# Row maxima of the feed-forward weights in units 1, 3 and 5 of each pair of heads, instead of 1, 4 and 7

## What is computed

```
q_r    = rope(q_hk @ w_kc_q) @ W_qr        # per head, rank 64
k_r    = kv @ W_kr                         # per head, rank 64
attn   = softmax(q_r @ k_r.T)              # 256 x 4096 per head
out    = concat((attn @ kv) @ w_kc_kv.T) @ Wo.T
```

```
scale = max(max(abs(row)) / 127, 1e-8)
q     = clip(round(row / scale), -127, 127)
```

## Time and profile before

| what | value |
|---|---|
| median of three runs | 1056.04 us |
| the profiled execution | 1053.18 us |
| its span, first to last instruction | 1051.5 us |
| PE / DVE / ACT / POOL busy | 94% / 70% / 55% / 28% |
| mean granted TensorE clock | 0.994 of full speed |

### The profile page before, as it was taken

How to read it: one execution, slowest core, us unless ns; L and a number is a source line. 1 busy time by engine, 2 the same in 40 slices (tenths; PEclk the granted TensorE clock), 3 DMA queues, 4 the chain that set the end, 5 groups by cost and what they waited for, 6 DMA issues and landing times.

```text
span 1051.5 us, 18010 instructions
## 1 busy us (share of the span) xinstructions
PE 990.6 (94%) x6641; PEld 788.4 (75%) x6641; DVE 732.6 (70%) x1434; ACT 575.1 (55%) x1251; POOL 291.2 (28%) x210
## 2 busy tenths in 40 slices
PE   7989989999998799999998999989899999989996
PEld 5545689999997576687787777878788787968653
DVE  3566456555553789788787888878877787658555
ACT  3445344444443320486776667767676777837633
POOL 6910144444442300000000422313225504013412
PEclk9999999999999999999999999999999999999999
DMA  8560076656632233201113347423323203083010
GB/s 269 130 242 1 4 231 245 213 210 209 209 121 82 83 95 101 71 29 28 52 46 54 61 92 103 91 53 77 76 58 95 72 1 96 8 295 162 1 66 21
DMA packets 65966, 109.18 MB, mean 104 GB/s; under 512 B 19393, under 2 KB 44129, under 8 KB 64738
## 3 DMA queue, kind: packets, MB, share of 16 engines
q1 hardware_dynamic: 65890, 108.17, 35.3%
HBM read 103.24 MB, written 4.91 MB: 103 GB/s over the span
## 4 chain that ended last, share of the span: by engine, by line
PE 76%; DVE 14%; ACT 5%; issue 2%; DMA 1%; POOL 1%; SPq 0%; DVEq 0%; ACTq 0%; POOLq 0%
PE PS L1618 14%; PE PS L1491 12%; PE PS L1607 9%; PE PS L1595 8%; PE PS L1510 5%; DVE scores L1145 3%; PE PS L1580 3%; PE PS L1710 3%; PE PS L1632 2%; PE PS L1339 2%; DVE pL L1198 2%; PE PS L1753 1%; ACT scores L832 1%; PE PS L1391 1%; PE PS L1550 1%
## 5 line engine op out<-in xcount | busy, mean ns | idle before, releaser
L1198 DVE TENSOR_TENSOR pL<-PS,pH 128x512 fp32r<-128x512 f32 x256 | 175.9, 687 | 66.0 <-ACT pH L856 65.5
L856 ACT ACTIVATE pH<-PS 128x512 fp32r<-128x512 f32 x256 | 151.7, 595 | 99.9 <-PE PS L1607 99.9
L832 ACT ACTIVATE scores<-scores,nmX 128x512 f32<-128x512 f32 x256 | 185.2, 723 | 26.3 <-DVE nmX L1149 26.3
L1145 DVE TENSOR_SCALAR_CACHE_REDUCE scores<-PS 128x512 f32<-128x512 f32 x256 | 172.6, 682 | 18.8 <-PE PS L1595 18.4
L1618 PE MATMUL PS<-pH,kvH 128*128 128x256 f32 x512 | 164.4, 321 | 7.4 <-ACT xnT L841 7.4
L1607 PE MATMUL PS<-ident,scores 128*128 128x128 f32 x1024 | 157.3, 276 | 4.5 <-DVE pL L1198 4.3
L1607 PEld LDWEIGHTS PS<-ident,scores 128*128 128x128 f32 x1024 | 117.0, 140 | 36.6 <-issue 16.4
L1618 PE MATMUL PS<-pL,kvH 128*128 128x256 f32 x512 | 143.9, 281 | 0.0
L1618 PE MATMUL PS<-pH,kvL 128*128 128x256 f32 x512 | 143.7, 281 | 0.0
L1618 PEld LDWEIGHTS PS<-pH,kvH 128*128 128x128 f32 x512 | 96.7, 189 | 11.6 <-issue 11.4
L614 POOL TENSOR_TENSOR xn<-xn,winvB 128x1024 f32<-128x1024 f32 (+1 forms) x17 | 39.6, 2330 | 211.0 <-DMA xn<-in_w1t 114.3
(11 more groups left out here) (305 smaller groups left out, 2250.1 us busy)
## 6 DMA issues: line engine op xcount, KB each, us to landing
rawG<-in_wg SPq DMA_DIRECT2D x16, 768.0 KB, 5.7
rawU<-in_wu SPq DMA_DIRECT2D x16, 768.0 KB, 7.2
rawD<-in_wd SPq DMA_DIRECT2D x16, 768.0 KB, 6.4
wrow<-in_w SPq DMA_DIRECT2D x11, 512.0 KB, 5.5
xn<-in_w1t SPq DMA_DIRECT2D x11, 512.0 KB
wturned<-turned SPq DMA_DIRECT2D x4, 1056.0 KB, 13.5
wb<-w_rows SPq DMA_DIRECT2D x32, 128.0 KB, 3.3
wqX<-in_wqX SPq DMA_DIRECT2D x16, 256.0 KB, 2.6
```

The source lines that it names most:

```text
L832: act.activation(at, at, ACT.Exp, bias=nmX[:, p % 2, h, q:q + 1], accum_out=csum[:, p % 2, NT * h + q, c:c + 1]).then_inc(exp_done, 1)
L856: act.activation(pH[:, i % 4], PS[:, 2 + i % 2, :].rearrange("p (k t) -> p k t", t=T), ACT.Copy).then_inc(pH_ready, 1)
L1145: dve.tensor_scalar(sp_[:, h, q, c * CH:(c + 1) * CH], PS[:, 4 * q + h, :], 1.0, None, ALU.mult, ALU.max, accum_out=cmax[:, h, q, c:c + 1] ...
L1198: dve.tensor_tensor(pL[:, i % 4], PS[:, 2 + i % 2, :].rearrange("p (k t) -> p k t", t=T), pH[:, i % 4].bitcast(F32), ALU.subtract).then_in ...
```

## The change

One constant is changed: the units in which a pair's three jobs are done.

```diff
-ROWS_AT = (1, 4, 7)
+ROWS_AT = (1, 3, 5)
```

## The result

The changed kernel takes 1051.1 us (median of 15 runs, 1044.57 to 1057.82), the kernel before 1056.37 us beside it (15 runs, 1052.86 to 1064.52). The ratio is 0.9943, 95% interval 0.9917 to 0.997: 5.3 us less by the medians. 1049.8 us and -6.2 us were forecast.

The account below looks back on a forecast made before the run. PE was taken to bound the kernel, busy 94% of the span and waiting for DVE only where pairs hand over. -7.89 + 0.34 + 0.3 + 1.05 = -6.2 us, from the median 1056.04 to 1049.8 us; range 1045.5 to 1055.5 us.

Parts of the forecast that it names:

- hand-over behind pair 0: Unit 7 and the next unit 0: without the job over 704 columns, 18.63 us falls to 16.58, 2.05 us less.
- hand-overs behind pairs 1 to 4: Unit 7 and the next unit 0: without the third job 1.47, 1.47, 1.45 and 1.45 us less, together 5.84.
- pair 0, units 1 to 6: A job over 704 columns makes a 7.03 us unit 7.37; unit 5 newly pays this, +0.34 us.
- meetings in unit 3, seen in unit 4: Pairs 2 to 4: POOL's first pass holds `wscale`, `add_out` makes PE 0.1 us late each, +0.3 us.
- meetings in unit 5, seen in unit 6: POOL's passes hold `wscale`: pair 2 loses 0.55 us, pair 3 nothing, pair 4 0.5; +1.05 us in all.
- rival 3: Hand-over behind pair 5 is short for another reason; only 0.47 us each is sure: -0.65 us, 1055.4 us; chance 0.13.
- b: DVE's lateness over the usual 0.46 us when the next unit begins; in unit 6, b over 0.75 us is lost.
- Meetings that cost nothing (1): Units 3 and 5: meetings with POOL miss or cost nothing; -7.5 us, 1048.5 us; chance 0.22.
- Meetings at their worst (2): Units 3 and 5: all six hold `wscale` for a whole first pass; +0.2 us, 1056.3 us; chance 0.10.
- That DVE is held for POOL's whole round (4): Units 3 and 5 of pairs 2 to 4: `wscale` loses a whole POOL round; +11.8 us, 1067.8 us; chance 0.05.
- The queues: Next job's row load, issued at most about 9.2 us into unit 3, lands at +15.9, with 3.0 us left.

Follow-up runs that it names:

- Experiments 1: Kernel before with only the second job moved, from unit 4 to unit 3; 1053.98 us, one execution.
- Experiment 5: Kernel before, jobs in units 1, 4 and 7, with the scale made as in experiment 3; 1059.76 us, one execution.
- Experiment 6: Kernel before without the two reductions of the job in unit 7, its small operations kept; 1051.32 us, one execution.
- Experiment 7: Kernel of experiment 3 with both halves behind part 3 in the jobs over 704 columns; 1049.07 us, ratio 0.9931 to the kernel before.
- experiment 9: Changed kernel timed again without new edits; 1052.14 us (12 runs), ratio 0.994 to the kernel before.
- experiment 3: Changed kernel with the scale clamped by a tensor_reduce and multiplied in the accumulator form, instead of the plain tensor_scalar; 1051.34 us, one execution.
- experiment 2: Kernel before with only the third job moved, from unit 7 to unit 6; 1049.4 us, one execution.

## Why the prediction was right

Term by term, in us of loop, from the two traces:

| Term | forecast | measured |
|---|---|---|
| hand-over behind pair 0 | -2.05 | -2.03 |
| hand-overs behind pairs 1 to 4 | -5.84 | -5.73 |
| pair 0, units 1 to 6 | +0.34 | +0.36 |
| meetings in unit 3, seen in unit 4 | 3 x 0.1 | 0.25 + 0.24 + 0.22 |
| meetings in unit 5, seen in unit 6 | +1.05 | +0.76 |
| sum | -6.2 | -5.9 (whole loop -6.05) |

*The hand-over.* It was read from a comparison that the trace of before held already, a pair with the job and one without. Experiments 1, 5 and 6 vary it three ways (job kept, 0.2 us added, 1.2 us removed), and the time followed nearly one for one. That rules out rival 3, by which the hand-over behind pair 5 was short for a reason of its own; so does the 16.6 us that the changed kernel shows behind all five pairs.

*Pair 0.* The three units with a job take 7.38 to 7.39, the others 7.03, as forecast. Experiment 7 shows that another place in the same unit does not help: with both halves behind part 3 the lateness comes out one unit later.

*Unit 3 was mis-sized by a factor of two.* The meeting came where it was put: `wscale` lasted 1.36 to 1.37 us (1.37 expected from 8.83 - 7.46), and in pair 4 the key matmul started 725.39 - 722.91 = 2.48 us into the unit against 2.35 to 2.36 without a hold, 0.12 us late where 0.1 was forecast; in pairs 2 and 3 it was 0.16 and 0.15. The step from the end of `add_out` to the matmul was 0.09 us (724.55 + 0.75 to 725.39), where the prediction had put 0.05. What it left out is that PE loses more than it waits. The matmul behind the wait takes 0.47 us instead of 0.40, and the next starts 0.31 us later instead of 0.23. With this 0.08 the 0.12 to 0.16 us are 0.20 to 0.24, nearly the 0.22 to 0.25 us of the table.

*Unit 5 came out near by luck; how a hold turns into time was right, when it comes was not.* The forecast had pair 2 lose 0.55 and pair 4 half of 0.95. In this execution POOL began pair 2's block 24.5 us after the start of unit 3, not 22.35, and `wscale` was through before it (611.94 against 612.95). The load was issued when forecast (13.62 us, forecast 13.8); what was wrong is the time of the load. The prediction took 8.55 us from the earlier trace rows and called it landing to first use, but it runs from the issue (651.04) to the first use, and here it was 10.9 us, in experiment 9 9.4 us. In the same way pair 4's block took 6.7 and 7.3 us where 5.16 was taken. So `wscale` met L615 there and not L617: b was 1.41, and b - 0.75 = 0.66. A restart as in unit 3, of 0.10, gives the 0.76 us seen. The timeline of pair 4's unit 6 shows the same steps: the tile of part 3 started 6.15 us into the unit (forecast 4.73 + 1.41 = 6.14), and the matmuls of q=1 at 6.89 us, 0.66 behind the 6.23 of before. In experiment 9 it was pair 2 that paid: b = 1.85, 1.10 plus 0.10, seen 1.19. Pair 3, put at 0, had b = 0.41 and lost nothing. So the formula (what DVE is late by, less 0.75) holds in all of these; which pair meets POOL is not settled by the program. The forecast of +1.05 lies between the 0.76 and 1.19 of two executions.

*The other rivals.* Meetings that cost nothing (1) would need unit 4 at 7.88; it took 8.10 to 8.14. Meetings at their worst (2) did not come, the longest `wscale` of the changed kernel being 2.02 us, once. That DVE is held for POOL's whole round (4) is excluded by 722.48 + 1.36, 738.47 + 1.58 and 611.80 + 2.02 = 613.82 beside 611.40 + 2.38 = 613.78: each hold ends with the pass it met.

The Trainium skill ("SBUF — State Buffer", Who interferes with whom) says that the loser of the shared port blocks for the whole instruction and that `tensor_reduce` is outside the lock. The trace agrees with the first: each hold ended within 0.04 us of the POOL pass that it met. It agrees with the second in that `wclamp` took 156 to 157 ns in all fifteen jobs of experiment 3, four of them in the middle of a POOL pass. In this kernel the holds were worth the 1.5 us of experiment 3.

*The queues.* The load of the next job's rows was issued 9.06 us into unit 3 in pair 2 (9.2 at most was forecast), and no job waited for rows: `wscale` stands 7.46 us into units 3 and 5 of pairs 1 to 4 in all cases.

*The total.* The medians differ by 5.3 us where the loop gives 6.05. The interval (0.9917 to 0.997, 3.2 to 8.8 us) holds both. The forecast of 1049.8 us is 1.3 us under the measured median, less than the scatter lets one tell. Whether something of the rest of the span belongs to the change is not settled: it took 569.7 us against 562.2, but experiments 1 (562.3, 11.5 us of its span at the lower clock) and 9 (569.5, 28.7 us) show both values with the same code there, and it goes with the time at the lower clock each time.

## What to carry to other kernels

Where one engine is busy in every stretch but one, look in that stretch for work of the engine it waits for that could stand elsewhere. In this kernel a moved instruction brought back what it removed there nearly one for one, and cost nothing where it went so long as its lateness stayed below what the next consumer forgave. Before moving, look for a unit in the trace that has the job and a twin that has not: their difference is the term. And judge a gain of half a per cent by the loop in which it lies as well as by the total, since the rest of the program may scatter by more than that.

## What the runs showed of the hardware

- A DVE `tensor_scalar` over 128x2 elements, 0.17 us alone, took up to 2.19 us beside a 2.4 us POOL pass (experiment 2), and each hold ended within 0.04 us of that pass's end, even when POOL's next pass followed at once. In experiment 3 the `tensor_reduce` of 128x4, the accumulator form over 128x2 and the `reciprocal` stood in the middle of a POOL pass in four jobs and took 0.15 to 0.17 us each, as in the other eleven.
- PE lost more than it waited: with its first key matmul 0.12 to 0.16 us late, the unit grew by 0.22 to 0.25 us. The matmul behind the wait took 0.47 us instead of 0.40, and the next one started 0.31 us behind it instead of 0.23.
- The granted clock outside the loop changes from run to run of the same program on this one core, and most of the scatter goes with it: over 15 runs, 13 us from the fastest (0.995) to the slowest (0.985), correlation -0.92.
